# A graph network's kernel: edges sorted by node degree and gathered row by row, against edges binned once in node order and summed through a dense count matrix

## The reference

```python
# mean aggregator
mean = segment_sum(x[src], dst) / max(deg, 1)
x = layernorm(x + relu(concat([x, mean]) @ W.T + b))
# relational layer: each edge sends a message both ways
m_fwd  = x[src] @ Wf[:, :D].T + edge_attr @ Wf[:, D:].T + b_fwd      # to dst
m_back = x[dst] @ Wb[:, :D].T + edge_attr @ Wb[:, D:].T + b_back     # to src
agg = segment_sum(concat([m_fwd, m_back]), concat([dst, src])) / count
x = layernorm(x + norm(leaky_relu(agg) + x, gamma, beta))
# two attention layers, 4 heads; self loops are added again
e = leaky_relu(s_src[src] + s_dst[dst]); p = exp(e - segment_max(e, dst)[dst])
h = segment_sum((p / denom[dst]) * h[src], dst) + bias
x = layernorm(x + h2 + x @ Wr)
# two mean aggregators, the best quarter of the nodes by score kept, two more
h = sage(relu(sage(x))); score = sigmoid(h @ w + b); keep the top N // 4 rows, others zero
x = layernorm(x + sage(relu(sage(kept))))
```

## Time and profile before

| what | value |
| --- | --- |
| time, median of 3 runs | 14164.51 us (14159.8 to 14166.87) |
| span of the profiled execution | 20080.3 us |
| instructions in it | 202669 |
| busy: POOL, PE, DVE, ACT | 9290.7, 7541.0, 5578.4, 2099.1 us |
| binning loop (scatters) | from 738 to 4238 us of the span |
| mean, relational phases | from 4342 to 12885 us |
| two attention phases | from 12885 to 16192 us |
| pool1 to pool4 and output | from 16230 to 20080 us |

### The profile page before, as it was taken

How to read it: one execution, slowest core, us unless ns; L and a number is a source line. 1 busy time by engine, 2 the same in 40 slices (tenths; PEclk the granted TensorE clock), 3 DMA queues, 4 the chain that set the end, 5 groups by cost and what they waited for, 6 DMA issues and landing times. The chain is left out here.

```text
span 20080.3 us, 202669 instructions
## 1 busy us (share of the span) xinstructions
PE 7541.0 (38%) x37110; PEld 5154.6 (26%) x37326; DVE 5578.4 (28%) x15372; ACT 2099.1 (10%) x4797; POOL 9290.7 (46%) x9643
## 2 busy tenths in 40 slices
PE   1344444435544555455445322200000035454544
PEld 1333333322222222222223222100000023332333
DVE  5333333322222222222220012355544520112011
ACT  0122222210111000000000000022222210000000
POOL 0344444454434444444444555555455544444454
PEclk9999999996666766766666555555555556666666
DMA  3000000011111111111122211212222222222222
GB/s 110 5 1 1 1 1 1 1 31 39 39 35 36 37 38 36 37 38 39 35 49 82 52 39 40 41 41 41 40 43 41 42 63 78 70 61 69 71 73 53
DMA packets 583176, 827.74 MB, mean 41 GB/s; under 512 B 367789, under 2 KB 441142, under 8 KB 568406
## 3 DMA queue, kind: packets, MB, share of 16 engines
q0 software_dynamic: 307808, 528.13, 12.8%
q10 hardware_dynamic: 180288, 279.31, 4.2%
q1 hardware_dynamic: 95030, 19.73, 0.5%
HBM read 759.54 MB, written 121.33 MB: 44 GB/s over the span
## 5 line engine op out<-in xcount | busy, mean ns | idle before, releaser
L940 POOL DMA_INDIRECT ring<-table_x,idx x2752 | 2628.6, 955 | 2781.1 <-PE bank L1007 1786.6
L1007 PE MATMUL bank<-ring,ident 128*128 x11904 | 2208.2, 366 | 2170.2 <-SPq L896 1800.6
L940 POOL DMA_INDIRECT ring<-edge_rows,idx x1856 | 1791.9, 965 | 2215.4 <-PE bank L1007 1500.3
L1007 PEld LDWEIGHTS bank<-ring,ident 128*128 128x128 f32 x11904 | 2094.5, 275 | 2276.7 <-issue 2273.6
L1025 PE MATMUL bank<-a_buf,ident_b 128*128 x5568 | 1802.3, 459 | 2146.9 <-issue 1303.4
L940 POOL DMA_INDIRECT ring<-table_att,idx x1856 | 1767.3, 952 | 1583.4 <-DVEq L1363 961.2
L1297 DVE TENSOR_SCALAR a_buf<-iota_w,in_piece 128x896 int16 x2784 | 1114.2, 457 | 2408.1 <-remote 1374.6
L395 PE MATMUL bank<-running,lo_Tf 128*128 128x100 f32 x3328 | 1079.1, 468 | 1470.5 <-DVE same L602 1154.2
L312 POOL DMA_INDIRECT slots_by_dst<-record,slot_no x832 | 799.3, 961 | 1628.2 <-DVEq L621 1363.6
L1025 PEld LDWEIGHTS bank<-a_buf,ident_b 128*128 128x128 bf16 x5568 | 630.4, 113 | 3316.3 <-issue 3151.8
L1050 PE MATMUL bank<-ident,ins 128*128 128x128 f32 x679 | 242.2, 382 | 3077.7 <-DVEq L1245 1232.6
(11 more groups left out here) (282 smaller groups left out, 9190.3 us busy)
## 6 DMA issues: line engine op xcount, KB each, us to landing
a_buf<-adjacency ACTq DMA_DIRECT2D x105, 1568.0 KB
edge_rows<-edge_attr ACTq DMA_DIRECT2D x10, 5312.5 KB, 100.8
ring<-table_x,idx POOLq DMA_INDIRECT x2752
adjacency<-counts ACTq DMA_DIRECT2D x147, 224.0 KB, 2.0
ring<-edge_rows,idx POOLq DMA_INDIRECT x1856
ring<-table_att,idx POOLq DMA_INDIRECT x1856
ring<-table_pool,idx POOLq DMA_INDIRECT x896
slots_by_dst<-record,slot_no POOLq DMA_INDIRECT x832
```

Source lines behind the costliest of these rows:

```text
L940: pool.indirect_dma_start(out=ring[:, j, g, 0:rows.shape[1]], out_offset=None, in_=rows, in_offset=bass.IndirectOffsetOnAxis(ap=idx[b][:, ...
L1007: mm = nc.tensor.matmul(ps_sum, ident[:], ring[:, entry, c, 0:D].rearrange("p a w -> p (a w)"), start=False, stop=False, skip_group_check= ...
```

## The change

It is a rewrite of the whole kernel in five blocks, with the nodes in the order of their numbers.

- Block a: each of 128 partitions holds 832 edges in a row. For each of the 49 source tiles DVE compares and scans once over all of them, which gives every edge a slot by source; POOL writes 832 records (832 indirect transfers). Since the edges come sorted by destination, the sums of the edge features by destination need no gather: they are streamed in 104 batches of 1024 edges, and for each pair of a batch and a destination tile that it touches (152 pairs) a one-hot is made and multiplied, and the rank of each edge at its node is counted.
- Block b: the whole count matrix, 49 lines x 14 windows of 448 columns. Each of the 686 cells is an outer product of one-hots of source and destination, over as many columns of 128 edges as hold edges of the cell (1495 in all for these inputs). Beside it run 896 gathers of edge features in source order and 162 pairs for their sums.
- Block c: mean aggregator by the dense product, relational layer (a second product, and 896 gathers of x with 162 pairs beside it).
- Block d: the attention with the edges on partitions: per layer 832 gathers and 152 pairs, each with one-hots between 1024 edges and 128 nodes.
- Block e: the four last aggregators by dense products, with the same search for the threshold.

Here the rows of L1899 to L1921 wait for PE, which spreads the nodes' values over the edges and adds the weighted rows; before, DVE added them itself. The diff, cut to its core:

```diff
-for k in range(2):
-    for q in range(QUAD):
-        pool.indirect_dma_start(
-            out=slots[k],
-            out_offset=bass.IndirectOffsetOnAxis(ap=slot_no[b][:, k, q:q + 1], axis=0),
-            in_=record[b][:, k, q, :], in_offset=None).then_inc(s_scatter[b], 16)
...
-for g in range(G):
-    rows, which = (edge_rows, 1) if source == "edges" else (tables[source], 0)
-    pool.indirect_dma_start(
-        out=ring[:, j, g, 0:rows.shape[1]], out_offset=None, in_=rows,
-        in_offset=bass.IndirectOffsetOnAxis(ap=idx[b][:, c + g, which:which + 1], axis=0),
...
-with pe.Fori(0, mine) as g:
-    hold(pe, s_landed, arrived + g + 1, s_held_pe)
-    entry = bass.ds((arrived + g) & (RING - 1), 1)
-    for c in range(G):
-        mm = nc.tensor.matmul(ps_sum, ident[:],
-                              ring[:, entry, c, 0:D].rearrange("p a w -> p (a w)"),
-                              start=False, stop=False, skip_group_check=True)
...
-for c in range(G):
-    for h, (lo, hi) in enumerate(HALVES):
-        mm = nc.tensor.matmul(
-            ps_piece[0][h], ident_b[:],
-            one_hot[:, bass.ds(b0 + c, 1), lo:hi].rearrange("p a w -> p (a w)"),
...
-hot.by(V.tensor_scalar(in_piece[:], src_idx[:, entry, :, 0].rearrange("p a g -> p (a g)"),
-                       float(-piece * WP), None, ALU.add))
-hot.settle(dve)
-dve.sem_inc(s_src_free, 1)
-hold(dve, s_hot_free, at_src + g + 1, s_held_dve)
-for c in range(G):
-    hot.by(V.tensor_scalar(one_hot[:, bass.ds(b0 + c, 1), :].rearrange("p a w -> p (a w)"),
-                           iota_w[:], in_piece[:, c:c + 1], None, ALU.is_equal))
...
-inner.by(V.tensor_tensor(raw[:], rows[:, :, HEADS * W_HEAD:],
-                         bc(tile_logit[:], 1, [P, G, HEADS]), ALU.add))
-inner.settle(dve)
-inner.by(V.scalar_tensor_tensor(logits[:, 0:G, :], raw[:], 0.2, raw[:], ALU.mult,
-                                ALU.max))
-inner.settle(dve)
-inner.by(V.tensor_reduce(peak[:], logits[:].rearrange("p g h -> p h g"), AX_X, ALU.max))
-inner.settle(dve)
-V.tensor_tensor(shifted[:], logits[:], bc(peak[:], 1, [P, G + 1, HEADS]),
-                ALU.subtract).then_inc(s_shift, 1)
-dve.wait_ge(s_probs, steps_at + g + 1)
-inner.by(V.tensor_copy(logits[:, G, :], peak[:]))
-inner.by(V.tensor_tensor(
-    weighted[:, 0:G, :].rearrange("p g (h c) -> p g h c", h=HEADS),
-    rows[:, :, 0:HEADS * W_HEAD].rearrange("p g (h c) -> p g h c", h=HEADS),
-    bc(probs[:, 0:G, :], 3, [P, G, HEADS, W_HEAD]), ALU.mult))
-inner.by(V.tensor_tensor(heads(weighted[:, G, :]), heads(att_acc[:]),
-                         bc(probs[:, G, :], 2, [P, HEADS, W_HEAD]), ALU.mult))
-inner.settle(dve)
-dve.sem_inc(s_free, 1)
-inner.by(V.tensor_reduce(att_acc[:], weighted[:].rearrange("p g f -> p f g"), AX_X,
-                         ALU.add))
-inner.settle(dve)
...
+def pick(b):
+    return st.by(V.tensor_scalar(is_tile[b % 3][:], tile_of[:], float(b), None, ALU.is_equal))
+made, scanned = pick(0), [st.k, st.k]
+for b in range(NT):
+    st.settle(dve, scanned[-2])
+    ahead = pick(b + 1) if b + 1 < NT else None
+    st.settle(dve, made)
+    scanned.append(st.by(V.tensor_tensor_scan(cum[:, b, :], ones_b, is_tile[b % 3][:], 0.0, ALU.mult, ALU.add)))
...
+for b in range(NT):
+    ahead = pick(b + 1) if b + 1 < NT else None
+    st.settle(dve, made)
+    dve.wait_ge(s_based, b + 1)
+    if b:
+        dve.wait_ge(s_taken, b)
+    V.copy_predicated(rank[:], is_tile[b % 3][:], based[b % 2][:]).then_inc(s_taken, 1)
...
+for c in range(TC):
+    pool.indirect_dma_start(
+        out=listed, out_offset=bass.IndirectOffsetOnAxis(ap=slot_no[:, c:c + 1], axis=0),
+        in_=record[:, c, :], in_offset=None).then_inc(s_scattered, 16)
...
+with pe.Fori(0, pairs_of(pe, in_end, NB, NB * NT) + 1) as i:
+    for h in range(2):
+        _, batch = code_of(pe, in_pairs, NB - 1, i * 2 + h)
+        unit = bass.ds(batch & 3, 1)
+        hold(pe, s_rows, batch + 1, s_held_pe)
+        pe.wait_ge(s_hot, i * 2 + (h + 1))
+        pe.wait_ge(s_prior_free, i * 2 + (h + 1))
+        for k in range(2):
+            part_of = is_dst_b[:, h, 4 * k:4 * k + 4, :].rearrange("p g f -> p (g f)")
+            nc.tensor.matmul(ps_prior[h][:, 512 * k:512 * k + 512], earlier_b, part_of, start=True,
+                             stop=False, skip_group_check=True)
+        for c in range(G - 1):
+            for k in range((c + 1) // 4, 2):
+                g0 = max(c + 1, 4 * k)
+                mm = nc.tensor.matmul(
+                    ps_prior[h][:, g0 * P:(4 * k + 4) * P].rearrange("p (g f) -> p g f", f=P), all_b,
+                    bc(is_dst_b[:, h, c, :], 1, [P, 4 * k + 4 - g0, P]), start=False, stop=True,
+                    skip_group_check=True)
+        mm.then_inc(s_prior, 1)
+        pe.wait_ge(s_hot_f, i * 2 + (h + 1))
+        pe.wait_ge(s_added, i * 2 + (h + 1))
+        for c in range(G):
+            mm = nc.tensor.matmul(ps_in[h], is_dst[:, h, c, :],
+                                  row_ring[:, unit, c, :].rearrange("p a f -> p (a f)"),
+                                  start=(c == 0), stop=(c == G - 1))
+        mm.then_inc(s_sum, 1)
...
+def cell(tile, window, q, more):
+    k0, n, at0 = cell_of(dve, q)
+    at0 = dve.snap(at0 + more)
+    with dve.Fori(0, n) as g:
+        hold(dve, s_hot_free, at0 + g + 1, s_held_dve)
+        at, k = bass.ds((at0 + g) & (HOT - 1), 1), bass.ds(nc.s_assert_within(
+            dve.snap(k0 + g), 0, COLS - 1, skip_runtime_bounds_check_because="k0 is at most COLS - n"), 1)
+        V.tensor_scalar(hot_src[:, at, :].rearrange("p a f -> p (a f)"), iota[:, bass.ds(tile * P, P)],
+                        key_id[:, k], None, ALU.is_equal)
+        V.tensor_scalar(hot_dst[:, at, :].rearrange("p a f -> p (a f)"), iota[:, window],
+                        key_dst[:, k], None, ALU.is_equal).then_inc(s_hot, 1)
...
+def cell(ps, n, at0):
+    def column(g, start):
+        hold(pe, s_hot, at0 + g + 1, s_held_pe)
+        at = bass.ds((at0 + g) & (HOT - 1), 1)
+        nc.tensor.matmul(ps, hot_src[:, at, :].rearrange("p a f -> p (a f)"),
+                         hot_dst[:, at, :].rearrange("p a f -> p (a f)"), start=start, stop=not start,
+                         skip_group_check=True).then_inc(s_hot_free, 1)
+    column(0, True)
+    with pe.Fori(0, n - 1) as g:
+        column(g + 1, False)
...
+def block(turn, slot, s, first, two):
+    pe.wait_ge(s_block[slot], turn * 16 + 16)
+    for piece in range(3):
+        if two is not None and piece < 2:
+            pair(two, piece)
+        for w in range(BH):
+            mm = nc.tensor.matmul(
+                psum[:, w, 0:WIN], parts[:, piece, s, :].rearrange("p a f -> p (a f)"),
+                a_ring[:, slot, w * WIN:(w + 1) * WIN], start=(first and piece == 0),
+                stop=not (first and piece == 0), skip_group_check=True)
+    mm.then_inc(s_used, 1)
...
+unit0 = pool.snap((n_pass * layer + k) * NB)
+for u in range(NB):
+    hold(pool, s_unit_free, unit0 + (u + 1), s_held_pool)
+    for g in range(G):
+        c = u * G + g
+        pool.indirect_dma_start(
+            out=row_ring[:, u % 4, g, :], out_offset=None, in_=table_att[layer],
+            in_offset=bass.IndirectOffsetOnAxis(ap=src_at[:, c:c + 1], axis=0)
+            ).then_inc(s_ring[u % 4][g % 4], 16)
...
+def spread(at, h):
+    pe.wait_ge(s_me, at + 1)
+    pe.wait_ge(s_ot, at + 1)
+    for c in range(G):
+        mm = nc.tensor.matmul(ps_spread[:, c, :, :].rearrange("p w f -> p (w f)"), from_dst[:, h, c, :],
+                              to_edge[:, h, :, :].rearrange("p w f -> p (w f)"), start=True, stop=True)
+    mm.then_inc(s_spread, 1)
+def gather_up(at, h):
+    pe.wait_ge(s_W, at + 2)
+    for c in range(G):
+        mm = nc.tensor.matmul(ps_out, is_dst[:, h, c, :], weighted[:, h, c, :],
+                              start=(c == 0), stop=(c == G - 1))
+    mm.then_inc(s_out, 1)
...
+def enter(at, first, h, q):
+    tile, batch = code_of(dve, in_pairs, NB - 1, q)
+    mine = bass.ds(batch * G, G)
+    A.begin(at)
+    A.by(V.tensor_scalar(key_near[:], key_now[:, mine], tile_base[:, bass.ds(tile, 1)], None, ALU.subtract))
+    A.by(V.tensor_tensor(rank_hot[:], bc(rank_now[:, mine], 2, [P, G, RANKS]),
+                         bc(iota_k[:], 1, [P, G, RANKS]), ALU.is_equal))
+    A.settle(dve)
+    hold(dve, s_rows, units_at[0] + batch + 1, s_held_dve)
+    V.tensor_tensor(ranked[:, h, :, 0:SLOTS].rearrange("p g (r f) -> p g r f", f=HEADS),
+                    bc(rank_hot[:], 3, [P, G, RANKS, HEADS]),
+                    bc(rows_at(batch)[:, :, FEAT:], 2, [P, G, RANKS, HEADS]), ALU.mult).then_inc(s_rs, 1)
+    if not first:
+        dve.wait_ge(s_out, at + 1)
+    V.tensor_tensor(is_dst[:, h, :, :], bc(key_near[:], 2, [P, G, P]), bc(iota_r[:], 1, [P, G, P]),
+                    ALU.is_equal).then_inc(s_hot, 1)
...
+def shift(at, h, q):
+    _, batch = code_of(dve, in_pairs, NB - 1, q)
+    dve.wait_ge(s_spread, at + 1)
+    C.begin(at)
```

(23 more changed lines are left out.)

3045 lines of the change are left out of this document (1877 added, 1168 removed).

## The result

| | before | after |
| --- | --- | --- |
| time, median | 14163.19 us (4 runs, 14159.8 to 14166.87) | 13968.83 us (4 runs, 13968.23 to 13968.99) |
| ratio, 95% interval | | 0.9863 [0.9849, 0.9877] |
| span of the profiled execution | 20080.3 us | 13967.2 us |
| busy: POOL, PE, DVE, ACT | 9290.7, 7541.0, 5578.4, 2099.1 | 4501.4, 8053.7, 5415.9, 1215.5 |

The change makes the kernel 1.4% faster; 6.8% was forecast, with the right sign. The profile of before is as long as in those two, so its span and waits can't be set against those of the profile after; what made it so long is answered under "The slow jobs".

A forecast was written before the change was run, and what follows sets the result against it. The prediction took POOL's descriptor work, about 85% of the time, to bound the kernel before. Its block terms, 1.35 + 3.9 + 2.0 + 3.83 + 2.07, gave 13.15 ms, forecast as 13,200 us, range 11,000 to 15,300.

The forecast's parts named there:

- What bounds the kernel before: Whole old kernel: POOL's descriptor work is about 85% of the time, 9619 indirect transfers at 1.25 us, 12.0 ms.
- The reading of the 1.42: Profiled execution of 20,080 us: sums up to 1.42 times as long there, the excess taken as a cost of recording.
- Its check: Same kind of sum for the kernel before: 13.5 ms against a median of 14.16, some 5% short.
- the likeliest case: Whole new kernel: 13,200 us, reaching from 12,300 to 14,000, chance 0.45.
- Block a, +0.13: Block a: 1.35 ms, 832 scatters at 1.27 us with DVE's pairs hidden under them; bounds 1.3 and 1.8.
- Block b, +0.40: Block b: 3.9 ms, a cell 4.5 us, a line 71 us with 8 us of pairs; bounds 1.4 and 5.5.
- Block d, +0.23: Block d: 3.83 ms, 304 pairs at 11.6 us plus 0.3 ms for starts, middle and norm; bounds 2.4 and 4.95.
- at the first DVE decides: Attention pair: with PE at 8.8 us, not 15.3, DVE's 11.6 us set the pair's time.
- Blocks c and e: Dense products at 4.0 us a block: c about 2.0 ms (bounds 1.9, 2.4), e about 2.07 (2.05, 3.7).
- Hidden sequencer: Rival, blocks b and d: register loads are shorter or hidden without recording, about 10.7 ms in all; chance 0.22.
- Gaps at a loop's end: Rival, block b: leaving each of 686 cell loops costs 2 us, 1.37 ms, 14.5 ms in all; chance 0.15.
- PE stays slow: Rival, block d: PE at low clock takes 15.3 us a pair, 1.12 ms more, 14.3 ms in all; chance 0.15.

The follow-up runs named there:

- the cuts: Kernel before, ended after binning, after rel_nodes_out or after the second attention layer: 3128.46, 8794.77 and 11495.91 us; rel_nodes_out again in a slow job 12824.18 us.
- b_tail: Kernel after, with SP in block b waiting for a ring place's release two units ahead of the arrival: 13873.84 us.
- d_early: Kernel after, with DVE's work for the next attention pair, except the one-hot, moved ahead of the peak: 13432.78 us, ratio to before 0.9485.
- d_slots: Kernel after, six of eight slots products per attention pair left out: 14739.68 and 14723.8 us in slow jobs; kernel after 15291.87 in the second.
- d_share: Kernel after, with three code loads per attention pair in place of five: 13964.62 us.
- b_const2: Kernel after, every count-matrix cell fixed to the first two columns, two of three loads left out: 14195.04 us in a slow job, then 12641.56 us.

## Why the prediction was wrong, step by step

What failed is that the sum has no place for an engine that waits for another or is held up by it: DVE for PE in blocks d and b, POOL beside DVE in block a. The long waits in the old profile were put down to the recording.

- **What bounds the kernel before**: right in the main. POOL issues at its own pace for 84 to 87% of the steps from one transfer to the next at the cuts. But the steps are longer on average than the median that was used (1.33 and 1.43 us against 1.25 and 1.27), so each stage comes out short. The reading of the 1.42 was wrong, as above. Had the result been taken in a slow job, the kernel before would have been at 20,000 us and the ratio at 0.77, far below the forecast.
- **Its check**: the same kind of sum fell 5% short for the kernel before. The forecast stayed at the bare sum and left the 5% to the edge of the likeliest case. 13.15 x 14.16 / 13.5 = 13.8 ms would have been 1.2% from the result. Much of that would have been luck: the kernel before is short by POOL's longer steps, the kernel after mainly by the waits named below.
- **Block a, +0.13**: the step of a scatter was mis-sized, 832 came each 1.49 us, not 1.27. 149 x 0.75 + 8 x 5.45 us = 0.16 ms of it lie in those that met the DVE operations above; the nearest row was one without such neighbours.
- **Block b, +0.40**: the cell, the least known term, was right (4.37 on average against 4.5). Mis-sized were the pairs at a line's end, 12.4 us in place of 8, of which 4.0 are DVE's wait for PE, put at nothing (a line is 73.5 us against 71: +0.12 ms); the end (0.57 in place of 0.37, 0.095 of it SP's order of waiting, by b_tail); and eight cells in a loop that runs even with nothing left over (0.07), not counted. The terms themselves add up to 3.95, which the prediction has as 3.9.
- **Block d, +0.23**: the step "at the first DVE decides" failed. DVE's sum was right (11.2 against 11.6), but the pair is a chain through both engines, 12.8 us. d_early and d_slots show it from both sides, d_share that DVE's own work is not the price. 304 x 1.2 us are 0.37 ms; starts, middle and norm, taken as 0.3, took less.
- **Blocks c and e**: right within 0.13 and 0.07 ms.
- **"Hidden sequencer"** is out, each load stands in the open at 0.72 us.
- **"Gaps at a loop's end"** is out too. The gap of 2.58 us is mostly the three loads, and b_const2, with two of them gone and the same loop ends, leaves a cell at 2.65 us. The rule of the Trainium skill on taken branches ("Runtime: NRT & Kernel Launch", "Instruction fetch mechanics") speaks of targets outside the pages loaded. Whether these branches have such targets no run here tells; the trace shows no stall at them.
- **"PE stays slow"** came in part. The granted clock was 0.76 in block d, and PE's 9.7 us a pair stand between the 8.8 and 15.3 of the two rows. Had all pairs been as the 73 with the short slots' products, the block would be 304 x (12.8 - 11.84) = 0.3 ms shorter, an estimate, about a quarter of the rival's 1.12. By this estimate most of what the chain cost above DVE's 11.2 us came with PE's lower clock in it.

## What to carry to other kernels

Where two engines answer each other, sum the chain from one wait to the next, not the busier engine; then move what needs no answer into the wait. That brought 4% here for one change of order, where two loads fewer a pair brought nothing until the wait was gone (0.12 ms then). Loads from memory into registers were serial time of the engine that made them, 0.72 us each. And when a check of the method on a known kernel falls short, find the stage and the term in which it does: here it was the mean step of the busy engine, taken as its median. Whether scaling a forecast by such a shortfall helps, one case doesn't show.

## What the runs showed that was not expected

- One kernel took 14,155 or 20,000 us by the job, and the ratio of two kernels changed with it: 0.9863 and 0.7652 for the same pair. POOL's pace (1.25 us a gather) and the length of register instructions did not change, the time between instructions did in some stretches.
- POOL's scatters of 0.96 us took up to 6.5 us when they began during a DVE operation with two inputs in SBUF.
- With six products left out PE's granted clock fell from 0.74 to 0.66, and other products of the same pair took longer (2.09 to 3.23 us): work taken from PE was not gained in full.
- A loop with a count from a register cost no gap at its end; each turn cost some 0.4 us of register work and branch.
